# Attention in query groups of 512 instead of 256, with one query buffer and a reordered last pair

## The reference

```python
qc = layernorm(x @ W_cq)                       # (S, 192)
q_nope, q_pe = split(qc @ W_q)                 # 16 heads, 128 + 64
k_pe, kv_nope = split(x @ W_ckv)
k_nope, v = split(layernorm(kv_nope) @ W_kv)
scores = [q_nope, rope(q_pe)] . [k_nope, rope(k_pe)] * scale
probs = softmax(causal(scores))
attn = probs @ v                               # (16, S, 128)
out = (attn + io) @ W_o                        # io: one row from the sparse branch
h = layernorm(x + out)
w = ternary(W_up), ternary(W_gate), ternary(W_down)
y = layernorm(h + (silu(h @ up) * (h @ gate)) @ down)
```

## Time and profile before

| | us |
|---|---|
| median of 3 runs | 682.4 (680.27 to 683.05) |
| the profiled execution | 682.62, span 680.8 |
| PE busy | 642.5 (94%), 4456 matmuls |
| PEld busy | 582.8 (86%) |
| DVE busy | 474.5 (70%) |
| ACT busy | 400.2 (59%) |
| POOL busy | 371.5 (55%) |
| granted TensorE clock, mean | 0.991 |

### The profile page before, as it was taken

How to read it: one execution, slowest core, us unless ns; L and a number is a source line. 1 busy time by engine, 2 the same in 40 slices (tenths; PEclk the granted TensorE clock), 3 DMA queues, 4 the chain that set the end, 5 groups by cost and what they waited for, 6 DMA issues and landing times.

```text
span 680.8 us, 14087 instructions
## 1 busy us (share of the span) xinstructions
PE 642.5 (94%) x4456; PEld 582.8 (86%) x4456; DVE 474.5 (70%) x1291; ACT 400.2 (59%) x934; POOL 371.5 (55%) x331
## 2 busy tenths in 40 slices
PE   7989999999999999999999999999999999889895
PEld 5878988899889988998889888988899888779895
DVE  3886467666766667666856586658666768997996
ACT  4775246744774485656564757456754767545552
POOL 6874278464744484456628472737454725521564
PEclk8989999999999999999999999999999999989999
DMA  7306232510461037103610343114510482000001
GB/s 224 126 2 148 70 69 63 125 57 1 110 147 54 0 92 162 54 0 92 140 53 23 92 94 67 54 46 93 115 54 0 112 239 74 10 1 1 1 17 47
DMA packets 23551, 49.85 MB, mean 73 GB/s; under 512 B 3168, under 2 KB 16352, under 8 KB 21600
## 3 DMA queue, kind: packets, MB, share of 16 engines
q1 hardware_dynamic: 22144, 47.82, 27.5%
q10 hardware_dynamic: 1376, 1.64, 0.7%
HBM read 16.94 MB, written 1.05 MB: 26 GB/s over the span
## 4 chain that ended last, share of the span: by engine, by line
PE 57%; DVE 14%; ACT 13%; issue 10%; POOL 4%; DMA 1%; ACTq 0%; DVEq 0%; POOLq 0%; SPq 0%
PE J L840 5%; PE J L842 4%; PE J L841 4%; PE J L873 4%; ACT Pb L1165 4%; PE J L889 3%; PE J L886 3%; ACT kvraw L1260 3%; PE J L885 3%; DVE SC L1375 3%; DVE PTl L1306 3%; PE SC L860 3%; PE SC L863 3%; PE SC L861 3%; PE SC L864 3%
## 5 line engine op out<-in xcount | busy, mean ns | idle before, releaser
L1306 DVE TENSOR_TENSOR PTl<-J,PTh 128x512 fp32r<-128x512 f32 (+1 forms) x192 | 102.8, 553 | 66.7 <-ACT PTh L1148 65.7
L1165 ACT ACTIVATE Pb<-SC,nm 128x128 f32<-128x128 f32 (+7 forms) x128 | 94.9, 742 | 56.6 <-DVE nm L1375 56.4
L1375 DVE CUSTOM_DVE_ANT_0 SC<-SC,mask 128x128 f32<-128x128 f32 (+7 forms) x128 | 97.1, 758 | 20.7 <-PE SC L864 19.6
L873 PE MATMUL J<-ident,Pb 128*128 128x128 f32 x576 | 88.0, 278 | 9.1 <-ACT Pb L1165 7.6
L1148 ACT ACTIVATE PTh<-J 128x512 fp32r<-128x512 f32 (+1 forms) x192 | 88.1, 492 | 7.2 <-PE J L873 6.6
L873 PEld LDWEIGHTS J<-ident,Pb 128*128 128x128 f32 x576 | 63.7, 141 | 19.1 <-ACT Pb L1165 8.9
L885 PE MATMUL J<-PTh,Vh 128*128 128x256 f32 x320 | 76.0, 273 | 0.8 <-DVE PTl L1306 0.8
L886 PE MATMUL J<-PTh,Vl 128*128 128x256 f32 x320 | 74.5, 280 | 0.0
L860 PE MATMUL SC<-KNh,QNh 128*128 128x128 f32 (+2 forms) x192 | 69.4, 361 | 0.1
L863 PE MATMUL SC<-KK,QS 128*128 128x128 f32 (+2 forms) x192 | 66.1, 344 | 0.0
L861 PE MATMUL SC<-KNl,QNh 128*128 128x128 f32 (+2 forms) x192 | 66.1, 344 | 0.0
(11 more groups left out here) (305 smaller groups left out, 1914.3 us busy)
## 6 DMA issues: line engine op xcount, KB each, us to landing
KK<-RK SPq DMA_DIRECT2D x30, 512.0 KB, 6.3
QS<-RQh SPq DMA_DIRECT2D x15, 256.0 KB, 7.5
QS<-RQl SPq DMA_DIRECT2D x15, 256.0 KB, 6.5
KX<-KX SPq DMA_DIRECT2D x14, 256.0 KB, 2.3
QX<-QX SPq DMA_DIRECT2D x14, 256.0 KB, 2.4
r_kv<-in_W_ckv SPq DMA_DIRECT2D x7, 384.0 KB, 3.6
r_o<-in_W_o SPq DMA_DIRECT2D x18, 128.0 KB, 2.1
r_qn<-in_W_qT SPq DMA_DIRECT2D x16, 128.0 KB, 2.1
```

The lines of the kernel that those rows point to most:

```text
L873: last = pe.transpose(o[:, tile(j - 4 * c)], Pb[i % 2][:, tile(j)], ident[:, :])
L1165: act.activation(Pb[i % 2][:, w], SC[i % 2][:, s], ACT.Exp, bias=nm[:, i % 2:i % 2 + 1], scale=-1.0, accum_out=sm[:, b, i:i + 1]).then_inc ...
L1306: dve.tensor_tensor(o, i, h.bitcast(F32), ALU.subtract).then_inc(done[kind], 1)
L1375: dve.tensor_tensor_reduce(out=SC[i % 2][:, s], in0=SC[i % 2][:, s], in1=mask[:, 128 * (7 - i):S], scale=-SCALE, scalar=HIGH, op0=ALU.add, ...
```

## The change

1. P x V works on 512 queries: two `pv` per head instead of four. `PTh` and `PTl` hold the transposed probabilities in blocks of 128 (`key_blocks`), so that one matmul can stream 512, 384, 256 or 128 queries. `ATh`, `ATl` become one buffer of 512 columns.
2. `QNh`, `QNl` have one buffer instead of two. The second half of the next head's `qn` moves to slot 7, behind the scores that still read the old one, and ACT gets a wait (`hold`) before the copy. `Wqnh`, `Wqnl` lie in free blocks of `PTh`, `PTl`.
3. The steps of every pair are placed anew, and `exp_at` puts several `exp` ahead of the slot's other steps.
4. In the last pair the ternary steps come a little earlier, `rowadd` moves from DVE to POOL, `ht 0`, `ug 0` and `ug 1` move from the pair's last slots into the epilogue, and the epilogue is rewritten.
5. At the start `W_cq` is loaded first and its high part is made by DVE, x's quarters change queues, six instead of four `qc` stand ahead of `kpe`, and the first `W_ckv` rest is split by ACT and DVE instead of POOL.

```diff
+DIAG = [0, 16]
+GAP = 26
+BLOCKS = 29
+def key_blocks(n):
+    i = TILE_OF[n]
+    g, ii, full = i // 4, i % 4, i >= 4 and n == CH0[i]
+    first, step, nb = (ii, 4, 4) if full else (DIAG[g] + ii, 3, ii + 1)
+    return slice(first, first + step * (nb - 1) + 1, step), nb
...
-        QNh.append(sb("QNh1", [128, S], F32R))
+        QNh.append(QNh[0])
...
-                add(4, True, *t(h, 3), ("wo", h, 0))
+                add(4, True, *t(h, 3))
...
-                add(5, True, ("pv", h, 1), *t(h, 4))
+                add(5, True, ("pv", h, 0), *t(h, 4))
...
-            exp_at = [[2, 2, 2, 2, 2, 2, 2, 2], [2, 2, 2, 2, 2, 2, 2, 2]]
+            exp_at = [[2, 0, 2, 2, 2, 1, 2, 1], [2, 0, 2, 2, 2, 0, 2, 1]]
...
-        EPILOGUE = [("wo", NH - 1, 2), *t(NH - 1, 7), one("ug", 2), one("ht", 1), one("m", 0), one("ug", 3), ("pv", NH - 1, 3),
+        EPILOGUE = [*t(NH - 1, 7), one("ht", 0), one("ln1", 1), ("pv", NH - 1, 1), one("ln1n", 1), one("ug", 0), one("m", 0),
...
-            gp.wait_ge(ld_cq, 16)
-            gp.tensor_copy(Wcqh[:, :, :], r_cq).then_inc(cq_hi, 1)
...
+                    if kind == "rowadd":
+                        gp.wait_ge(done["rwt"], 1)
+                        gp.wait_ge(done["wo"], count("wo", NH - 2, c))
+                        a = acc[:, 2 * c:2 * c + 2, :]
+                        rb = row[:, :].rearrange("p (a n) -> p a n", a=1).to_broadcast([128, 2, D])
+                        gp.tensor_tensor(a, a, rb, ALU.add).then_inc(row_added, 1)
...
+                if i % 4 == 0 and not first:
+                    pe.wait_ge(done["qn"], count("qn", h, i // 4))
...
+                full = [(j, slice(0, 512), slice(512 * j, 512 * j + 512)) for j in range(4 * g)]
+                diag = [(4 * g + r, slice(128 * r, 512), slice(128 * (DIAG[g] + 4 * r), 128 * (DIAG[g] + 3 * r + 4))) for r in range(4)]
+                if g == 1:
+                    pe.wait_ge(hi["tc"], NCH * h + CH0[7] + 1)
+                for j, z, q in full:
+                    mm(o[:, z], lhsT=Vh[b][:, j, :], rhs=PTh[:, q], start=j == 0, stop=False)
+                    mm(o[:, z], lhsT=Vl[b][:, j, :], rhs=PTh[:, q], start=False, stop=False)
...
+                        if not (isinstance(u, int) and u == 0):
+                            hold(act, sc_ready, T * (u - 1) + 4 * c + 4)
                         copy(QNh[b][:, half(c)], o[:, :]).then_inc(hi["qn"], 1)
...
+            dve.wait_ge(ld_cq, 16)
+            dve.tensor_copy(Wcqh[:, :, :], r_cq).then_inc(cq_hi, 1)
             run(placed(PRO_DVE), 0)
```

More of the change, by code:

```diff
@@ L181, in attention_and_mlp @@
         Pb = [sb(f"Pb{i}", [128, S]) for i in range(2)]
-        PTh, PTl = sb("PTh", [128, T, 256], F32R), sb("PTl", [128, T, 256], F32R)
-        ATh = [sb(f"ATh{i}", [128, 256], F32R) for i in range(2)]
-        ATl = [sb(f"ATl{i}", [128, 256], F32R) for i in range(2)]
+        PTh, PTl = sb("PTh", [128, BLOCKS * 128], F32R), sb("PTl", [128, BLOCKS * 128], F32R)
+        ATh, ATl = sb("ATh", [128, 512], F32R), sb("ATl", [128, 512], F32R)
+        Wqnh, Wqnl = [X[:, 128 * GAP:128 * GAP + 256].rearrange("p (r n) -> p r n", r=2) for X in (PTh, PTl)]
         wip = KX[:, :, :]
@@ L363, in late_steps @@
[L363 to L371 removed]
+                    add(0, True, ("wld", 0, 0), ("wld", 0, 1), ("wabs", 0, 0))
+                    add(1, True, ("wabs", 0, 1))
+                    add(2, True, ("wtot", 0, 0))
@@ new lines, in mlp_steps @@
+                    add(3, True, ("wld", 0, 2), ("wabs", 0, 2), ("tern", 0, 0))
+                    add(4, True, ("wabs", 0, 3), ("tern", 0, 1), ("wosp", 2, 0))
+                    slots[5].insert(0, ("tern", 0, 2))
+                    add(5, True, ("wtot", 0, 1), ("tern", 0, 3))
+                    slots[6].insert(0, ("tern", 0, 4))
+                    add(6, True, ("wabs", 0, 4), ("tern", 0, 5), ("wabs", 0, 5), ("wosp", 3, 0))
+                    add(7, True, ("tern", 0, 6), ("wtot", 0, 2))
+                else:
+                    slots[0].append(("tern", 0, 7))
+                    add(1, True, ("tern", 0, 8))
+                    add(2, True, ("rowadd", 0, 0), ("tern", 0, 9))
+                    add(3, True, ("rowadd", 0, 1), ("tern", 0, 10))
+                    add(4, True, ("rowadd", 0, 2), ("rowadd", 0, 3), ("tern", 0, 11))
@@ L372, in head_steps @@
+            def late_steps():
+                add(6, True, ("ln1", 0, 0))
+                add(7, True, *t(h, 6), ("wo", h, 1), ("ln1n", 0, 0))
+            add(0, tail, *t(m, 7))
+            add(0, b == 0 or last, ("wo", m, 1))
+            add(1, True, ("pv", m, 1))
             add(1, True, *t(h, 0))
@@ L386, in head_steps @@
                 add(5, more, ("kv", 1, 0))
-                add(5, True, ("pv", h, 1), *t(h, 4), ("qn", n, 1))
+                add(5, True, ("pv", h, 0), *t(h, 4))
                 add(6, more, ("kv", 1, 1))
-                add(6, True, *t(h, 5), ("wo", h, 1))
+                add(6, True, *t(h, 5))
+                add(6, more, ("wo", h, 0), ("wo", h, 1))
                 add(6, last, ("rw", 2, 0))
                 add(6, more, ("kv", 1, 2))
+                add(7, True, ("qn", n, 1))
                 add(7, more, ("kv", 1, 3))
-                add(7, True, ("pv", h, 2), *t(h, 6))
+                add(7, last, ("wo", h, 0))
+                add(7, True, *t(h, 6))
             else:
@@ L418, in head_steps @@
                 add(4, first, ("io", 1, 0))
-                add(6, more, ("qn", n, 1))
                 add(4, more and not first, ("io", 1, 0))
-                add(6, True, *t(h, 5), ("wo", h, 1))
+                add(6, True, *t(h, 5))
+                add(6, last, ("wo", h, 0))
                 add(5, more, ("rw", n, 0))
                 add(6, more, ("skip", 0, 0))
-                add(7, more, ("wosp", h + 2, 0), ("wqn", h + 2, 0))
-                add(7, True, ("pv", h, 2), *t(h, 6))
+                add(7, more, ("qn", n, 1), ("wo", h, 0), ("wosp", h + 2, 0), ("wqn", h + 2, 0))
+                add(7, not last, *t(h, 6))
             if last:
@@ L1552, in run @@
                         dve.tensor_copy(row[:, :], o[:, 0:D]).then_inc(done["rwt"], 1)
[L1553 to L1558 removed]
                     if kind == "pv":
[L1560 removed]
+                        lo("pv", u, c, ATl[:, :], o[:, :], ATh[:, :])
                     if kind == "wo":
```

131 lines of the change are left out of this document (54 added, 77 removed).

## The result

The changed kernel takes **687.38 us** (median of 7 runs, 686.68 to 688.07) against 681.99 for the kernel before on the same chip: ratio **1.0073**, 95% interval 1.0053 to 1.0093. It is slower by 5 us, where 674 was forecast and 681 was the end of the range. Timed a second time on another chip, the ratio was 1.0077 (1.0057 to 1.0098).

A forecast was written before the change was run, and what follows sets the result against it. PE was taken to bound the kernel: its stream plus the holes in it. 682.6 us profiled - 6.4 (P x V) - 0 - 0 - 1.5 (last pair, epilogue) - 0.8 (start) = 673.9, stated as 674; range 660 to 681.

The forecast's parts named there:

- P x V, -6.4: P x V in groups of 512 queries: fewer matmuls per head, 36 instead of 60, saving 6.4 us in all.
- One query buffer, 0: Sharing one query buffer: the new waits on ACT and PE would already be satisfied, so cost nothing.
- Order of the middle pairs, 0: Middle pairs: shorter waits behind exponentials and new holes from lost cover cancel; ends -2.0 and +2.9 us a pair.
- new holes that I had summed to 2.95: Middle pair: new waits at `wo`, `kt`, tile 3's transposes and the passage to the next head, 2.95 us together.
- the first rival: Middle pairs: the new order pays too, 13 us more gained, about 661 us in all; chance 20%.
- First pair, 0 (-1 to +1.5): First pair: 0.8 us lost as a `wo` stops covering the side branch's wait, balanced by second-head waits; net nought.
- waits in the pair's second head like those above: First pair's second head: waits like the middle pairs', set against the 0.8 us lost at the side branch.
- Last pair and epilogue, -1.5 (-3 to +4): End: moving additions to POOL frees 2.9 us of DVE, a new last-tile hole costs 1.2; 1.5 us gain taken.
- The start, -0.8: Start: earlier `W_cq` load and a DVE cast bring PE's first product 0.8 us sooner; ends nothing and 1.2.
- cover gone: Tiles 2 to 4 lose PE work as cover, 0.9 us more waiting in every head: 688 us; chance 8%.
- The lock rival: Last pair: POOL's additions hold DVE through shared ports, losing 3.2 us more than gained: 678.6 us; chance 8%.
- all three rivals on the order: Order pays, about 661 us (20%); width and reorder win nothing, about 680 (14%); lost cover slows it, 688 (8%).

The follow-up runs named there:

- e3: c3 with ternary steps earlier in the last head, POOL's additions behind them all, and `wtot 2` after that head's first scores: 676.66 us, 0.9901 of the kernel before.
- g1: c3 with P x V in groups of 256 queries, before's order and epilogue, and additions on DVE in the last pair alone: 671.43 us, 0.9826 of the kernel before.
- a3: The changed kernel with every exponential back at place 2 of its slot, as before: ratio 1.0032 to the kernel before.
- c3: The changed kernel with new exponential places in middle pairs only and a P x V group ahead of the side branch's wait: 677.90 us, 0.9929 of the kernel before.
- d1: The changed kernel with 23 useless matmuls in PE's three longest waits of the last head and epilogue: 682.98 us, 1.0008 of the kernel before.
- b1: The kernel before with nothing but the new start of the change: ratio 0.9947 to the kernel before.
- a1: The changed kernel with the four additions of the bias row back on DVE: ratio 1.0047 to the kernel before.

## Why the prediction was wrong

- **P x V, -6.4: right.** A head's groups take 1.86 + 4.65 = 6.51 us from start to start at the median; before 0.72 + 1.35 + 2.07 + 2.77 = 6.91. That is 0.40 a head, 6.4 in all, and 576 matmuls. (The rows had summed to 6.82 and 6.46; the rest up to 6.4 was an allowance, and it fits.) Both groups that met the low clock (6.13 and 6.87 us) come on top, which the term had not.
- **One query buffer, 0: right in the middle pairs, not free at the end with this order.** It is why `qn 1` can't stay in slot 5 of the last pair (ACT would wait there for scores of a later tile), and `wtot 2` then waited 2.3 us for its bank. But e3 removed that wait and won 1.4 us by the middle values, and g1 kept the buffer and lost nothing.
- **Order of the middle pairs, 0: too low.** The pairs gained 8.6 us, of which P x V explains 0.8 x 6 = 4.8. The rest, 0.6 a pair, is the order. In the pair of the earlier trace rows PE's starts were late at six places by 2.8 us in sum; after, by 1.5 at four. The new holes that I had summed to 2.95 are mostly not there; none is over 0.5 us. By the sign that I had named, PE's waits for `Pb` and `kvraw` (3 us a pair by my forecast, 1 by the first rival), the first rival was right in the loop: 0.7 us in two places. a3 puts the exponentials' places at 1.0 us a pair, so the other moves cost some 0.4. So the pair came out at 70.3 us, inside the bounds I had set.
- **First pair, 0 (-1 to +1.5): wrong, +4.4, and about +7 for the same work.** The loss of the `wo` ahead of the side branch was seen and sized at 0.8. In its place: the wait grew to 2.06 us, the clock fell to 0.72 behind it (c3 shows both go with a cover), and the exponential ahead of P x V's copy cost 1.7 us of waiting at 110 and about as much again by the clock (a3). With both mended (c3) the stretch still takes 88.6 us, 0.3 more than before with 2.6 us less work in it; what the rest is stays open. This is the step where I said that "waits in the pair's second head like those above" would be repaid.
- **Last pair and epilogue, -1.5 (-3 to +4): the step that failed, +12.6, and about +10 for the same work.** Three things were missing. (1) I priced the new hole at the last tile at 1.2 us; it is 2.2, with 1.8 at `ht` behind it, and 2.8 at tile 3 that I had taken for relieved. (2) I gave POOL's lateness 0.2 us; DVE's relief of 2.9 us was 0.9 after the stretched ternary steps. DVE did become less than full (13.63 of 17 us), the sign that I had named for this step being right, but because it waited. (3) I costed every hole at its own length. The clock made P x V take 2.2 us more, and some 4 us in all (d1). Above these stands what g1 showed: narrow groups in this pair, with before's order and the additions on DVE, are worth 6.5 us against c3, and no order tried with wide ones got under 136 us.
- **The start, -0.8: too small, -3.6 (b1).** The first product came 1.4 to 1.8 us earlier and not 0.8, and the projections no longer ran at a low clock. That low clock, 0.72 from 8 to 14 us, stood in the trace of before, in a window that I had not read.

Of the rivals, "cover gone" (688 us, 8%) named the right total for a wrong reason: it put 0.9 us of waiting into every head, and the middle pairs waited less than before. The lock rival was right in its mechanism and small in its price: 2.0 us of DVE and not 6.1. The earlier trace rows had one row for it and one against. Here, of three ternary steps beside POOL's TENSOR_TENSOR, the two that started 0.06 us after it took 1.75 us, and the one that started first kept 0.74. Of five beside a TENSOR_SCALAR, the two that started some 0.12 us after it (563.04 and 574.61 us) took 1.1, the others 0.74; where the step was first (572.33 us), the comparison took 2.00 in place of 1.56. The Trainium skill (SBUF — State Buffer, section Who interferes with whom) says that a DVE instruction with two SBUF inputs contends with a GpSimd instruction that reads SBUF; the additions agree with it, one side or the other losing about 0.5 to 1.0 us, and the comparisons only in part, since a step that started 0.7 us after one lost nothing.

The chances were off because all three rivals on the order treated the kernel as one stretch. The profile had said otherwise: DVE 16.20 of 17 us busy in the last pair, 48.57 of 71.90 in the middle.

## What to carry to other kernels

Here larger pieces of PE work paid where the other engines had slack and cost where one of them was full, so choose the size and the order by stage: one table for loop and ends cost 1.1% here, and narrow groups in the last pair alone another 1%. Price a long wait of PE (here two microseconds) at its length plus the slow clock that may follow it, and look for a long dense group directly behind it. Before pricing a stretch between two marks, count whether the same work lies between them. Before moving work to a free engine, see what it waits for and what then queues behind it.

## What the runs showed of the hardware

- Of 59 waits of PE of 1.9 to 3.2 us (idle time in brackets; fourteen profiles, without a1, the first 5 us and the last stretch behind 660 us), 52 were followed by six microseconds at a mean granted clock of 0.50 to 0.78, the lower of the two levels being half (1.2 GHz), though PE was then mostly busy. Behind the other seven it was 1.00. The same wait can go either way: behind 1.90 us near 600 us it was 0.72 in the kernel before (602 to 608) and 1.00 in b1. Some shorter waits were followed by it as well (1.68 us at 8.30 in the kernel before). What decides it isn't settled. Useless matmuls in three such waits kept the clock at full speed (2.4 GHz) behind them (d1), and that kernel was 0.6% faster.
- At the low level a matmul of 512 columns starts every 0.43 us, against 0.23.
- A DVE operation with two SBUF operands took 1.75 us instead of 0.74 when a TENSOR_TENSOR of POOL had started 0.06 us before it. Where the DVE operation had started 0.16 us before, it kept 0.74 us and POOL's took 1.73 in place of 1.27.
